# Last stage of a two-layer kernel: sum blocks grouped by three, the narrow projection in two copies side by side

## The reference, cut to what matters

```python
r = jnp.einsum('bhwc,cd->bhwd', x, Wr) + br                       # 64 -> 16, "narrow projection"
r = jax.nn.relu((r - mean) * jax.lax.rsqrt(var + BN_EPS) * gamma + beta)
w = jnp.einsum('bhwd,dk->bhwk', r, Ws) + bs                       # 16 -> 9 * 16
w = w.reshape(B, H, W, G, KK)[:, :, :, :, None, :]
xi = jnp.einsum('bhwc,cf->bhwf', x, Wi) + bi
xp = jnp.pad(xi, ((0, 0), (pad, pad), (pad, pad), (0, 0)))
patches = jnp.stack([xp[:, i:i + H, j:j + W, :] for i in range(K) for j in range(K)], axis=3)
patches = patches.reshape(B, H, W, G, F // G, KK)
out = jnp.sum(w * patches, axis=-1)
...
x = x + _L1_conv_ref(_gn(x), ...)
```

## Time and profile before

| what | value |
|---|---|
| median of 3 runs | 698.71 us (698.58 to 699.46) |
| the profiled execution | 699.03 us, its span 697.2 us |
| TensorE, VectorE, ScalarE, GpSimd busy over the span | 94%, 79%, 41%, 25% |
| last stage | from about 465 us to the end |
| L1453, products on VectorE | 288 instructions, 179.3 us busy |
| L711, expansions on TensorE | 288 records, 97.0 us busy |
| L727, sums on TensorE | 1280 records, 79.7 us busy |
| L677, narrow projection on TensorE | 64 records, 31.9 us busy |

### The profile page before, as it was taken

One profiled execution on the slowest core, in us unless ns is written; L12 is line 12 of the kernel. 1 busy time (PEld: TensorE's weight loads), 2 busy tenths in 40 slices (PEclk: granted clock), 3 DMA queues, 4 the chain that ended last, 5 costly groups with the idle time before them and its releaser, 6 DMA issues.

```text
span 697.2 us, 14818 instructions
## 1 busy us (share of the span) xinstructions
PE 652.6 (94%) x6176; PEld 271.0 (39%) x6176; DVE 549.3 (79%) x896; ACT 289.0 (41%) x372; POOL 173.9 (25%) x157
## 2 busy tenths in 40 slices
PE   7878999699999999999999999979999999999993
PEld 7433333223333333333333334424444444444441
DVE  5698957968987988995565789956888888888881
ACT  3753713122322422143002410025677777777742
POOL 2100400008202800450051200212343243243241
PEclk9989999899999999999999999997999999999997
DMA  9920000000000000000000000000111211211212
GB/s 333 206 48 1 2 1 1 1 1 1 3 1 1 2 1 1 1 2 1 1 14 2 1 2 1 1 1 1 27 35 32 60 32 32 61 32 31 61 31 61
DMA packets 54478, 19.66 MB, mean 28 GB/s; under 512 B 51122, under 2 KB 51860, under 8 KB 54420
## 3 DMA queue, kind: packets, MB, share of 16 engines
q1 hardware_dynamic: 54132, 18.57, 10.9%
q10 hardware_dynamic: 288, 0.21, 0.1%
HBM read 10.39 MB, written 8.39 MB: 27 GB/s over the span
## 4 chain that ended last, share of the span: by engine, by line
PE 75%; DVE 13%; ACT 2%; issue 1%; POOL 1%; DVEq 0%; POOLq 0%; ACTq 0%
PE conv L635 36%; PE conv L711 11%; PE att L727 11%; PE att L452 5%; PE att L677 4%; DVE comb L1239 3%; DVE xpad L1158 2%; PE att L699 2%; PE conv L601 2%; PE att L689 2%; PE att L510 1%; DVE x L1215 1%; DVE x L1216 1%; DVE x L1223 1%; DVE stats L1253 1%
## 5 line engine op out<-in xcount | busy, mean ns | idle before, releaser
L635 PE MATMUL conv<-xpad,comb 64*64 64x512 f32 x2592 | 289.8, 595 | 2.8 <-DVE x L1223 2.7
L1453 DVE TENSOR_TENSOR x<-conv,x 128x512 f32<-128x512 f32 x288 | 179.3, 684 | 32.9 <-PE conv L711 31.5
L635 PEld LDWEIGHTS conv<-xpad,comb 64*64 64x64 f32 x2592 | 100.7, 134 | 168.4 <-issue 156.7
L1239 DVE SCALAR_TENSOR_TENSOR comb<-experts,wsel,comb 128x576 f32<-128x576 f32 (+1 forms) x138 | 113.7, 892 | 10.6 <-ACT comb L833 10.5
L711 PE MATMUL conv<-rstack,wse 98*128 98x512 f32 x288 | 97.0, 452 | 3.2 <-POOL rstack L1569 2.6
L833 ACT ACTIVATE comb<-experts,wsel 128x576 f32<-128x576 f32 (+2 forms) x52 | 37.2, 770 | 111.5 <-PE conv L635 69.7
L727 PE MATMUL att<-x,cmp 64*32 64x512 f32 x1280 | 79.7, 596 | 0.0
L711 PEld LDWEIGHTS conv<-rstack,wse 98*128 98x128 f32 x288 | 50.8, 194 | 61.5 <-DVE x L1453 44.4
L1158 DVE SCALAR_TENSOR_TENSOR xpad<-att,x 128x1024 f32<-128x1024 f32 x46 | 54.0, 1215 | 20.4 <-PE att L510 20.2
L1576 POOL TENSOR_TENSOR x<-x,xin 128x1024 f32<-128x1024 f32 x16 | 38.4, 2397 | 124.1 <-ACT x L973 124.1
L843 ACT ACTIVATE x<-conv,bias 128x512 f32<-128x512 f32 x40 | 25.2, 682 | 83.6 <-PE conv L635 83.6
(11 more groups left out here) (179 smaller groups left out, 602.9 us busy)
## 6 DMA issues: line engine op xcount, KB each, us to landing
x<-in_x SPq DMA_DIRECT2D x32, 256.0 KB, 5.1
out<-comb SPq DMA_DIRECT2D x32, 256.0 KB, 3.2
experts<-in_We SPq DMA_DIRECT2D x1, 1152.0 KB
wide<-in_c_wide SPq DMA_DIRECT2D x1, 192.0 KB, 5.5
x<-in_c_sum SPq DMA_DIRECT2D x1, 160.0 KB
small<-in_c_small ACTq DMA_DIRECT2D x1, 142.5 KB, 3.5
map_sel<-in_c_map SPq DMA_DIRECT2D x1, 128.0 KB
wr<-in_Wr SPq DMA_DIRECT2D x6, 4.0 KB
```

Source lines behind the costliest of these rows:

```text
L635: last = nc.tensor.matmul(conv[own[to], h, HW * rows:HW * rows + HW], comb[own[rows], q % 2, n, tap(t)], xpad[own[rows], 2 * (q % 2) + n, ...
L1239: v.scalar_tensor_tensor(comb[:, q % 2, n, cols], experts[:, e, cols], wsel[:, p % 2, j + QP * n, e:e + 1], comb[:, q % 2, n, cols], ALU.m ...
L1453: v.tensor_tensor(img(prod[i])[:, rows, :], img(conv[:, unit, :])[:, rows, :], xip[s][:, kh + 16 * h:kh + 16 * h + 16, kw:kw + W], ALU.mul ...
```

## The change

Three things change, all in the last stage:

- The narrow projection has 64 columns (`wr` is 128x64, two copies of 32) and each half of the pixels goes to its own 64 partitions of PSUM. ScalarE evicts it in two relus of 64x512 into `r64`, copies 64 rows to `rstk`, and makes the third copy in an instruction of its own, with its own semaphore `third_ready`, for which the first expansion waits.
- The sum rounds of a pair stand in two places and not in three: rounds 0 and 1 before xi's projection, rounds 2, 3 and 4 in the next pair. Expansions 6, 7 and 8 then follow each other.
- The parameters of the batch norm (`rsc`) cover 128 rows, and `wr` is loaded by four DMAs, not six.

```diff
-        wr = sb("wr", [128, AR])
+        wr = sb("wr", [128, 2 * 32])
...
-        r96 = flat[0:AR, 8 * S:9 * S]
+        r64 = flat[0:64, 8 * S:9 * S]
...
-                   for n in range(2) for a in range(PARTS)]
+                   for n in range(2) for a in range(2)]
...
-            def project(k, s, m, weights, rows):
+            def project_r(k, s, m):
+
                 if not (isinstance(m, int) and m == 0):
                     eng.wait_ge(misc_free, m)
                 eng.wait_ge(xn_ready, k + 1)
                 for h, cols in halves():
-                    last = nc.tensor.matmul(att[0:rows, 1, cols], weights, xn[s][:, cols], start=True, stop=True)
+                    last = nc.tensor.matmul(att[own[h], 1, cols], wr[:, :], xn[s][:, cols], start=True, stop=True)
                 last.then_inc(misc_full, 1)
...
                 if i == 0:
                     eng.wait_ge(rstk_ready, k + 1)
+                    eng.wait_ge(third_ready, k + 1)
...
                 if not first:
+                    add_up(k - 1, 2)
                     add_up(k - 1, 3)
                     add_up(k - 1, 4)
                 expand(k, s, 2)
                 expand(k, s, 3)
                 if not last:
-                    project(k + 1, 1 - s, m, wr[:, :], AR)
+                    project_r(k + 1, 1 - s, m)
                 expand(k, s, 4)
                 expand(k, s, 5)
                 add_up(k, 0)
+                add_up(k, 1)
                 if not last:
                     project_xi(k + 1, 1 - s, m + 1)
                 expand(k, s, 6)
                 expand(k, s, 7)
-                add_up(k, 1)
-                add_up(k, 2)
                 expand(k, s, 8)
                 if not first:
                     turn_back(k - 1, m if last else m + 2)
...
-                nc.scalar.activation(r96, att[0:AR, 1, :], ACT.Relu, bias=rsc[:, 3:4], scale=rsc[:, 1:2])\
-                    .then_inc(misc_free, 1)
+                for h, cols in halves():
+                    done = nc.scalar.activation(r64[:, cols], att[own[h], 1, cols], ACT.Relu, bias=rsc[own[h], 3:4], scale=rsc[own[h], 1:2])
+                done.then_inc(misc_free, 1)
                 eng.wait_ge(misc_free, m + 1)
-                nc.scalar.activation(rstk[s][0:AR, :], r96, ACT.Copy).then_inc(rhi_ready, 1)
+                nc.scalar.activation(rstk[s][0:64, :], r64, ACT.Copy).then_inc(rhi_ready, 1)
+                nc.scalar.activation(rstk[s][64:AR, :], r64[0:32, :], ACT.Copy).then_inc(third_ready, 1)
```

More of the change, by code:

```diff
@@ L177, in build @@
         earlier = earlier.rearrange("p (a b) -> p a b", a=K)
-        rpar = rpar[0:AR, :]
         pair_avg, same_image = (packed(wide, n * 128, 128) for n in range(2))
         first_sel = packed(wide, 2 * 128, 2 * C).rearrange("p (m c) -> p m c", m=2)
-        rsc = sb("rsc", [AR, 4])
+        rsc = sb("rsc", [128, 4])
         stats = sb("stats", [128, NP, 2, 6])
@@ L273, in build @@
         rhi_ready = sem("rhi_ready")
+        third_ready = sem("third_ready")
         rstk_ready = sem("rstk_ready")
@@ L753, in involve @@
                     turn_back(k - 1, m if last else m + 2)
-            project(0, 0, 0, wr[:, :], AR)
+            project_r(0, 0, 0)
             project_xi(0, 0, 1)
@@ L766, in _ @@
                 involve(k, k % 2, last=(k == NP - 1))
+            add_up(NP - 1, 2)
             add_up(NP - 1, 3)
@@ L1489, in _ @@
             eng.wait_ge(nmr_ready, 2)
-            v.tensor_tensor(rsc[:, 2:3], rsc[:, 0:1], mhalf[0:AR, 0:1], ALU.pow).then_inc(setup_pool, 1)
+            v.tensor_tensor(rsc[:, 2:3], rsc[:, 0:1], mhalf[:, 0:1], ALU.pow).then_inc(setup_pool, 1)
             eng.wait_ge(setup_pool, 2)
@@ L1568, in r_lo @@
                 eng.wait_ge(rhi_ready, k + 1)
-                v.tensor_tensor(rstk[s][32:64, :], r96[32:64, :], rstk[s][32:64, :].bitcast(F32), ALU.subtract)\
+                v.tensor_tensor(rstk[s][32:64, :], r64[32:64, :], rstk[s][32:64, :].bitcast(F32), ALU.subtract)\
                     .then_inc(rstk_ready, 1)
```

## The result

The changed kernel takes 717.59 us (median of 5 runs, 715.59 to 718.11), the kernel before 698.71 (5 runs, 698.05 to 699.46): 1.0266 times as long, 95% interval 1.0254 to 1.0278. Its profiled execution took 717.59 us with a span of 715.8, against 699.03 and 697.2.

A forecast was written before the change was run, and what follows sets the result against it. TensorE bounds the kernel before; after the change, the turn back waiting for xi's eviction was to end last. Thirteen longer periods +15.1, start +0.2, last pair +0.2 make 15.5 on 698.71: 714.2 us, range 707.5 to 720.

The forecast's parts named there:

- E2: Third of a pair's nine expansion blocks, counted from zero; its start is t = 0 for the forecast's steps.
- VectorE lets E5's second half go: Sixth expansion of a pair: its second half waits for VectorE's products, until 3.07 us.
- A0: First sum block of a pair, after the sixth expansion: forecast to start at 3.50 us, ScalarE's emptied sums hidden.
- the rival in which they don't: Narrow projection's copies run one after the other: period 14.41 us, 719 to 720 us in all; chance 0.12.
- E4: Fifth expansion of a pair, right after the narrow projection r, which was priced at 0.88 us.
- the turn back's start: Turn back waits for xi's eviction, ending at 9.22 us; weights 0.06 later, matmuls 0.23 after that, at 9.51.
- the clock falls: Rival: the granted clock drops for some pairs, about 10 us each, 725 us and up; chance 0.04.
- E7: Eighth expansion of a pair, in the group of three expansions between xi's projection and the turn back.
- E8: Ninth and last expansion of a pair, directly ahead of the turn back; xi's eviction was forecast to reach past it.
- The start: Everything up to the third pair's E2: +0.2 us forecast, with −1.5 to +1.5 as bounds.
- only VectorE's chain binds: Rival: VectorE's products alone set the last stage's period, 13.69 us, giving 707.9 us; chance 0.12.
- faster: Rival: TensorE stays the bound of the last stage, own work 12.17 us a period, some 685 to 687; chance 0.06.

The follow-up runs named there:

- the experiment without the wait: Changed kernel with two of the four pieces of xi's eviction left out (second image of a pair): 710.45 us, 1.017 of the kernel before.
- r_only_late: Kernel before plus the two-copy narrow projection, sums unmoved, ScalarE making the third copy behind xi's eviction: 695.94 us, 0.9956 of the kernel before.

## Why the prediction came out as it did

The direction and the mechanism were right: 714.2 predicted, 717.6 measured, in the range of 707.5 to 720. The growth was 18.9 us and not 15.5. That it is no further off is in part luck: the period was forecast too long (−2.0 us), and the sum had nothing for the falls of the clock (+3.1 and +1.4).

| step, us after E2's start | predicted | measured |
|---|---|---|
| VectorE lets E5's second half go | 3.07 | 3.08 |
| A0 | 3.50 | 3.51 |
| xi | 5.25 | 5.25 |
| ScalarE done with the third copy | 6.38 | 6.39 |
| xi's eviction starts | 6.43 | 6.43 |
| period | 14.17 | 14.02 |
| VectorE's chain alone | 13.69 | 13.67 |

(Measured from E2 at 590.08; the third copy ends in this pair at 595.42 + 1.05, the eviction starts at 596.51.)

Of the signs that the prediction named, three lie just outside their bounds: the period is 14.02 and not 14.1 to 14.2, r's four records take 1.08 and not 1.0, and TensorE is busy for 94% of the period (13.18 of 14.02) and not for 80 to 90%. The others came as named.

The prices taken from neighbouring rows held: two relus in 1.56 for 1.54, the copy of 32 rows 1.05 for 1.06, three blocks 2.73 for 2.74. For r, the copies run side by side, four records in 1.08 us: the rival in which they don't is out. The page TensorEngine Tiling of the Trainium skill (Key Properties) has tiles compute at once, and here that is shown for 128x64. E4 starts 1.01 us after r, not 0.88, and r 1.13 us after E2 where it was 1.03. These 0.23 us may be the changes of tiling, which no run measures by themselves; nothing waited for them, as E5's second half waits for VectorE behind them.

Where the 3.1 us between the predicted span of 712.7 and the measured one of 715.8 lie (starts are those of the chain that ended last):
- The period: 13 x (14.02 − 14.17) = −2.0. The step was the turn back's start. I had its matmuls 0.23 us behind its weights and E0 0.81 behind them, as in the earlier trace rows, where the weights come early. After a wait, weights and matmuls start together and E0 follows 0.92 later.
- Two falls of the clock at turn backs: +3.1. This was my rival "the clock falls", and I mis-sized it on both sides: I put it at 0.04 and at 10 us for a pair. It happened in two pairs of thirteen and cost 1.5 us each. The step that failed was to judge it by the busy share of a whole period: 13.2 us of 14.0 are busy. What stood ahead of the falls in the loop was one idle stretch, 0.66 us behind E7 and E8, which themselves wait for VectorE; the prediction had this wait, but gave it no price beyond its length.
- The start: third pair's E2 at 506.02, not at 503.8: +2.2. Most is a third fall of the clock (1.4). The rest is r's saving at the start, which was hardly used. The first pair's E0 waits for GpSimd's low part, which started 0.55 us earlier (468.90 for 469.45) but took 2.71 us for 2.33: E0 came at 471.87, after 471.93 before. (The longer low part overlaps VectorE's work on `wse`, 468.05 to 469.42, and the one before started as that ended; the cause isn't shown.) In the second pair r took 1.98 us for 3.62 at the lower clock, as forecast, but E4 started only 0.66 us earlier (477.91 for 478.57).
- The last pair: −0.2.

The rival "only VectorE's chain binds" is not what the kernel does, but what it would do next: the experiment without the wait gives 13.67. The rival "faster" had TensorE's own period at 12.17 and left out that E5 waits for VectorE; with both other obstacles gone it is 12.75. The cause of the slowdown by parts: the moved sums alone give +1.27 a period, the projection alone +0.15, both +1.01.

## What to carry to other kernels

Count how much work the consumer has in store before grouping blocks that it doesn't need: with four halves of 0.60 us in PSUM, a group of two blocks (1.87 us) costs 0.5 us of pause and one of three (2.74 us) 1.37. A saving on the engine that bounds the kernel is kept only if the steps that it brings to other engines don't stand ahead of something that this engine waits for; here, moving one copy of 1.06 us behind an eviction turned no gain into 0.4%. And a saving reaches the period only as far as the next wait: 0.26 us of 0.84 here. Where TensorE begins to wait in a tight loop, the wait can cost more than its length, through the clock: two waits of 0.64 us cost 1.5 us more each.

## What the runs showed of the hardware

- The granted clock fell to the lower level for some 3 us after idle times of only 0.64 to 0.66 us, in stretches in which TensorE was busy for 1.58 of 2.40 us before, while it was busy for 94% of the period. With 0.21 us idle ahead of the turn backs it didn't. It fell as well in the last pair of `r_only_late` (0.52 from 672.4 to 675.8), behind idle times of 0.15 us and less, and, in the kernel with half of the eviction, at the start of the stage (0.53 from 488.4 to 491.8, with no idle time above 0.10 us in the 3 us before). So no least idle time is shown.
- It fell at some turn backs and not at others with the same rows before them: two here (613.38 and 685.04, 71.66 us apart), four with the moved sums alone (44.4 us apart), three with the copy by DMA (503.09, 574.75 and 646.41, 71.66 us apart in both distances).
- Two 128x64 float32 matmuls with different columns of the array and all 128 rows run side by side: four records in 1.08 us against 1.88 for the 128x96 ones.
